# The order of a scan's loads in one DMA queue: the next pair's diagonals of B ahead of the present pair's C

## The reference

```python
x = x + 0.5 * ffn(layernorm(x))                 # y = xn @ int4(kernel) + bias + (xn @ a) @ b
x = x + mamba(layernorm(x))                     # below; it normalizes once more inside
x = x + 0.5 * ffn(layernorm(x))
# mamba, D_INNER = 512 channels d, D_STATE = 64 states s, 512 times t
x_ssm, z = split(h @ Win);  x_ssm = silu(conv4(x_ssm) + conv_b)
dt = softplus(x_ssm @ dt_w + dt_b);  A = -exp(A_log);  Bt = x_ssm @ Bp;  Ct = x_ssm @ Cp
state[d,s] = state[d,s] * exp(dt[t,d] * A[d,s]) + dt[t,d] * x_ssm[t,d] * Bt[t,s]
y[t,d] = sum_s state[d,s] * Ct[t,s]
out = x + ((y + x_ssm * D) * silu(z)) @ Wout
```

## Time and profile before

| | us |
|---|---|
| median of 3 runs | 5358.86 |
| the profiled execution | 5360.27 |
| its span, first to last instruction | 5358.5 |
| VectorE busy | 4882.4 (91%) |
| GpSimd busy | 5020.4 (94%) |
| TensorE busy, matmuls | 4832.5 (90%) |
| ACT busy | 3908.3 (73%) |
| 512 loads of C, median to landing | 5.3 |
| 512 loads of B, median to landing | 6.2 |

### The profile page before, as it was taken

One profiled execution on the slowest core, in us unless ns is written; L12 is line 12 of the kernel. 1 busy time (PEld: TensorE's weight loads), 2 busy tenths in 40 slices (PEclk: granted clock), 3 DMA queues, 4 the chain that ended last, 5 costly groups with the idle time before them and its releaser, 6 DMA issues.

```text
span 5358.5 us, 189344 instructions
## 1 busy us (share of the span) xinstructions
PE 4832.5 (90%) x85070; PEld 2903.5 (54%) x85070; DVE 4882.4 (91%) x4595; ACT 3908.3 (73%) x6661; POOL 5020.4 (94%) x2310
## 2 busy tenths in 40 slices
PE   4798989989999998989989999898999989899887
PEld 2455555555555555555555555555555555555554
DVE  1699999999999999999999999999999999999996
ACT  4767787777778677786777778777786777867564
POOL 0699999999999999999999999999999999999997
PEclk8899999999999999999999999999999999999999
DMA  6465665756556566665656556565665656557553
GB/s 174 161 170 192 180 185 190 177 199 180 188 185 182 192 171 202 179 184 189 180 197 181 189 179 181 197 172 194 183 176 192 173 198 171 190 183 180 187 188 115
DMA packets 578860, 976.04 MB, mean 182 GB/s; under 512 B 294881, under 2 KB 328450, under 8 KB 510466
## 3 DMA queue, kind: packets, MB, share of 16 engines
q1 hardware_dynamic: 313858, 961.82, 56.1%
q10 hardware_dynamic: 264192, 2.11, 3.4%
HBM read 875.74 MB, written 88.08 MB: 180 GB/s over the span
## 4 chain that ended last, share of the span: by engine, by line
PE 35%; POOL 26%; DVE 21%; issue 10%; ACT 4%; DMA 3%; SPq 0%; DVEq 0%; ACTq 0%; POOLq 0%
POOL H L618 23%; DVE H L528 18%; PE pUB L685 14%; PE Y L709 12%; PE pP L649 4%; PE pP L643 3%; DVE cv L479 2%; DMA Bd<-scratch_diag 2%; ACT dA L362 2%; PE pA L723 1%; POOL duo L605 1%; POOL dto L599 1%; POOL lnv L594 1%; ACT L362 1%; PE pA L729 1%
## 5 line engine op out<-in xcount | busy, mean ns | idle before, releaser
L618 POOL TENSOR_TENSOR H<-H,Cb 128x1024 f32<-128x1024 f32 x2048 | 4783.7, 2372 | 151.3 <-DVE H L528 141.9
L528 DVE TENSOR_TENSOR_SCAN H<-dA,pUB 128x512 f32<-128x512 f32 x4096 | 4640.1, 1199 | 244.1 <-PE pUB L685 219.8
L362 ACT ACTIVATE dA<-DT,w_negA 128x512 f32<-128x512 f32 x4096 | 2623.9, 713 | 1226.0 <-DVE H L528 1222.2
L685 PEld LDWEIGHTS pUB<-Bd,UT 64*64 64x64 f32 x65536 | 1867.5, 134 | 1439.1 <-DVE H L528 683.7
L685 PE MATMUL pUB<-Bd,UT 64*64 64x128 f32 x65536 | 2236.7, 275 | 413.3 <-DVE H L528 320.9
L709 PE MATMUL Y<-H,w_ident 64*64 64x512 f32 x16384 | 1971.2, 596 | 5.9 <-POOL H L618 4.9
L709 PEld LDWEIGHTS Y<-H,w_ident 64*64 64x64 f32 x16384 | 596.7, 135 | 611.1 <-issue 599.7
L643 PE MATMUL pP<-hT,w_Win 128*128 128x512 f32 x512 | 265.8, 643 | 19.8 <-DVE cv L479 12.6
L649 PE MATMUL pP<-U,w_dt_w 128*128 128x512 f32 x512 | 259.7, 631 | 5.1 <-DVE absv L542 3.7
L362 ACT ACT_TABLE_LOAD x178 | 228.4, 1283 | 6.5 <-DVE H L528 3.3
L479 DVE SCALAR_TENSOR_TENSOR cv<-pP,w_conv_w,cv 128x511 f32<-128x511 f32 (+2 forms) x192 | 139.2, 725 | 30.0 <-ACT cv L300 29.7
(11 more groups left out here) (80 smaller groups left out, 1745.1 us busy)
## 6 DMA issues: line engine op xcount, KB each, us to landing
Cb<-scratch_c SPq DMA_DIRECT2D x512, 1024.0 KB, 5.3
Bd<-scratch_diag SPq DMA_DIRECT2D x512, 512.0 KB, 6.2
scratch_diag<-H SPq DMA_DIRECT2D x16, 1024.0 KB, 15.2
scratch_z<-zo SPq DMA_DIRECT2D x64, 256.0 KB, 5.7
scratch_dt<-dto SPq DMA_DIRECT2D x64, 256.0 KB, 6.4
scratch_ut<-uto SPq DMA_DIRECT2D x64, 256.0 KB, 5.6
DT<-scratch_dt SPq DMA_DIRECT2D x64, 256.0 KB, 5.1
UT<-scratch_ut SPq DMA_DIRECT2D x64, 256.0 KB, 5.6
```

The costliest lines, as they stand in the source:

```text
L362: last = nc.scalar.activation(dA[:, n % DAR, j, :], DT[:, k, :], ACT.Exp, scale=c["negA"][:, k, GS * blk + j:GS * blk + j + 1])
L528: last = nc.vector.tensor_tensor_scan(H[:, u % HR, 2 * i + j, :], dA[:, n % DAR, 2 * i + j, :], pUB[:, i, :].rearrange("p (t s) -> p s t", ...
L618: nc.gpsimd.tensor_tensor(h[:, j:j + 2, :], h[:, j:j + 2, :], Cb[:, blk % 2, j:j + 2, :], ALU.mult).then_inc(times_c, 1)
L685: last = nc.tensor.matmul(out, UT[rows, k, j * P + h * HP:j * P + h * HP + HP], Bd[rows, blk % 2, i, j * P:(j + 1) * P].rearrange("p (t s) ...
```

## The change

load_block is split in two. load_b(b, seq + 1) stands where load_block stood, with the same wait, and asks for the next pair's diagonals. load_c(b, seq) stands behind it and asks for the C of the *present* pair; it waits until GpSimd has multiplied unit 2 * seq - 3, the last one that used that buffer, and that the batch's C has been stored (c_st). The C of the pass's last pair is asked for in step 62, and that of its first pair in step 0 rather than in step 62 of the pass before. The stores of dt move from steps 34, 40, 48, 56 to 35, 41, 49, 57, those of u from 42, 50, 58, 62 to 43, 51, 57, 63: odd steps, in which no B or C is loaded.

```diff
--- before.py
+++ after.py
@@ -29,7 +29,7 @@
 SPS = {"load x": (0,), "load 2": (10, 14), "load 0": (46, 54), "load r": (2,), "store z": (6, 12, 16, 22), "store C": (26,),
-       "store dt": (34, 40, 48, 56), "store u": (42, 50, 58, 62), "load z": (28, 29, 36, 37), "store out": (48,), "store r": (52,)}
+       "store dt": (35, 41, 49, 57), "store u": (43, 51, 57, 63), "load z": (28, 29, 36, 37), "store out": (48,), "store r": (52,)}
 ACTS = {"tap": (2, 7, 12, 17), "u": (5, 10, 15, 20), "z": (5, 10, 15, 20), "BC": (24,), "B": (26,),
         "store B": (27, 28, 29, 32, 33, 34, 35, 38), "dt": (30, 36, 44, 52), "log": (31, 37, 45, 53), "turn u": (40, 48, 56, 61),
         "keep u": (57, 59), "norm 1": (3, 4, 6, 11), "norm c": (22, 23, 26, 29), "norm 2": (39, 42, 43, 47, 49),
@@ -207,13 +207,18 @@
                                      w["Win"][:, DI + ch:DI + ch + HP].rearrange("(k p) m -> p k m", p=P)).then_inc(k_big, 16)
                         sp.dma_start(c["Wout"][side:side + HP, tile, :], w["Wout"][ch:ch + HP, :]).then_inc(k_big, 16)
-            def load_block(b, seq, units):
+            def load_b(b, seq, units):
                 blk = seq % NBLK
                 sp.wait_ge(forced, at(2 * units))
                 diag = dram["diag"][bass.ds(b % 2, 1), (2 * blk + 1) * EL:(2 * blk + 3) * EL].rearrange("o (i p f) -> p (o i) f", p=P, f=T)
                 sp.dma_start(Bd[:, seq % 2], diag).then_inc(d_in[seq % 2], 16)
-                sp.wait_ge(times_c, at(2 * units))
+
+            def load_c(b, seq):
+
+                blk = seq % NBLK
+                sp.wait_ge(c_st, at(16 * b + 16))
+                sp.wait_ge(times_c, at(2 * (GN * b + 2 * seq - 2)))
                 rows = dram["c"][bass.ds(b, 1), GS * blk + 1:GS * (blk + 1) + 1, :].rearrange("o s t -> o (s t)")
                 sp.dma_start(Cb[:, seq % 2].rearrange("p s t -> p (s t)"), rows.to_broadcast([P, GS * T])).then_inc(c_in[seq % 2], 16)
@@ -252,7 +257,9 @@
                         sp.wait_ge(x1_done, at(2 * a))
                         sp.dma_start(X[:, :, :], tokens_of("x", a)).then_inc(x_in, 16)
                     if scan and n % 2 == 0 and seq < 2 * NBLK - 1:
-                        load_block(b, seq + 1, GN * b + n)
+                        load_b(b, seq + 1, GN * b + n)
+                    if scan and n % 2 == 0:
+                        load_c(b, seq)
                     if scan and n in when["load 2"]:
                         load_du(b, 2 + when["load 2"].index(n))
                     if close and n in when["load r"]:
@@ -283,8 +290,7 @@
                         load_du(q, when["load 0"].index(n))
                     if proj and n == GN - 2:
                         sp.wait_ge(d_st, at(16 * 2 * NJ * (q + 1)))
-                        sp.wait_ge(c_st, at(16 * q + 16))
-                        load_block(q, 0, GN * q - 2)
+                        load_b(q, 0, GN * q - 2)
             sp.dma_start(X[:, :, :], tokens_of("x", 0)).then_inc(x_in, 16)
             constants()
```

## The result

The changed kernel is slower. Its runs take 5403.65 to 5438.38 us, median 5431.77, against 5359.90 for four runs before; the ratio is 1.0132, 95% interval 1.0097 to 1.0168. The forecast was 5367, "no change that can be told", in a range that ended at 5412. The profiled execution of the changed kernel (5403.65 us) is the quickest of its runs, with a granted clock of 0.977; the others have 0.970 to 0.972.

A forecast was written before the change was run, and what follows sets the result against it. GpSimd's work and the scan were taken to bound the kernel by turns. Per pass, -1.9 us (B(0) sooner) and +2.4 (GpSimd late at unit 38) gave +0.5, over 15 joints +7.5: 5367 us, range 5322 to 5412.

The forecast's parts named there:

- no change that can be told: Whole kernel: the forecast outcome, 5367 us, own range 5340 to 5390, chance 0.50.
- Item 1: Late units: B leaves before C's wait, closing VectorE holes such as 1.58 us at unit 60; worth nothing by itself.
- the sign in the prediction, under 30: Profile after the change: TensorE's waits for B were to fall from 119 us to under 30.
- Item 2: Start of the next pass: B(0) asked for and landing sooner, 1.9 us a pass gained, bounds 0.5 and 3.7.
- Item 3: Units 8 to 38: C behind B is 1.5 us late, free there; C(19) costs 0.8 us at unit 38.
- Item 4: Units 27 to 35, among diagonals' stores: C late 4.5 us, 2.1 worked off, 2.4 left at unit 38.
- They don't add, the greater holds: At unit 38: of the 2.4 us lag and C(19)'s 0.8 us only the larger counts.
- Item 5: Stores of dt and u at their new steps: 0 us, bounds -0.3 and +0.5 us a pass.
- Late C wins: Slower rival: C(14) to C(17) late in units 28 to 34, 3.3 us a pass, 5409 us; chance 0.29 with its kin.
- its own sign: Sign of the slower rival: GpSimd begins unit 38 over 4 us after that unit's first two scan rows.
- The new wait of VectorE behind TensorE's sums: Sign at L709 that the forecast's ground is wrong: GpSimd's lag would have reached VectorE; no size given.

The follow-up runs named there:

- e8: e7 with the next pass's B(0) (first diagonals) asked for ahead of C(31), the pass's last C; 5319.03 us, ratio 0.9895 to the kernel before.
- e7: Changed kernel with C behind the next B only for pairs 0 to 2 and 24 to 31, other C a pair ahead; 5354.60 us, ratio 0.9965.
- e3: Changed kernel with the eighth store of B's diagonals moved from step 38 to step 42; 5435.96 us, ratio 1.0113.
- r1: The changed kernel run and profiled again, unaltered, on another chip; 5459.44 us, ratio 1.0153.
- e2: Kernel before with only the new steps of the dt and u stores, old order of the loads; 5382.77 us, ratio 1.0014.
- e9: Changed kernel with the next pass's B(0) asked for ahead of C(31); 5399.58 us, ratio 1.0053.
- e10: Kernel before with one difference, the next pass's B(0) asked for ahead of C(31); 5376.45 us, ratio 1.0000.
- e5: Changed kernel with all eight stores of B's diagonals moved to steps 39 to 46; 5474.06 us, ratio 1.0181.

## Why the prediction was wrong, point by point

- *Item 1, B no longer behind C's wait, worth nothing by itself: right as far as it goes.* The 119 us of the earlier trace rows are waits of TensorE's weight loads; its matmuls waited 65.7 us for B, some 8 of them in front of unit 64. (In the pass that the prediction read, it took TensorE to be held by its own work, since the row says "issue"; B(0) landed 0.1 us before TensorE's start there, too.) After, the waits in front of the other units are gone and those in front of unit 64 are 50 us: the sign in the prediction, under 30, failed. The lead brings VectorE to unit 63 4.3 us sooner. Its main use comes with e8's swap, where it is worth 3.4 us a pass (joint 1 of e7 against e8).
- *Item 2, B(0) sooner, 1.9 us a pass: the size right, the parts not.* Joint 1 gained 1.6 to 1.7 us (8.8 to 7.15, 7.1). The request is 0.5 us sooner, as computed, but the landing only 0.8 us and not 1.5; the rest is VectorE's lead, which the item had named for some of the passes.
- *Item 3, C late in the quiet part: its size right there, wrong at unit 38.* From B's request 6.8 us, as computed. But "There the room is from 2943.70 to 2949.70, 6.0 us, and C(19) lands after 6.8: 0.8 us" took the quiet price in a place where the eighth store of diagonals goes out 1.05 us ahead of B(20). The prediction's own text spoke of "seven of eight from unit 27 to 35" and gave the eighth, at step 38, no price. Measured: lands at 11.1 to 11.6, not 6.8 (e3, without the store: 7.4). This is the step that failed.
- *Item 4, lag from the stores' part: 2.4 us at unit 38 predicted, 3.5 and 3.3 measured* (after, r1) as GpSimd's end of unit 37 (9.2 and 9.0 against 5.7). The start was mis-sized by little: GpSimd is 5.9 us behind the scan at unit 28 (before 0.6, medians), so 5.3 against 4.5. What was wrong is the working off: I counted 2.1 us of before's idle time as free for it, but new waits for C fill part of it (0.54 and 0.80 us above, at units 30 and 32). At unit 36 it is still 5.3 us behind (before 0.4).
- *"They don't add, the greater holds":* so far right; joint 2 is the later of the two. But the greater was C(19), and joint 2 4.8 to 5.5 us later than before, not 2.4.
- *Item 5, the stores' steps, 0: right* (e2, at the edge of its interval).
- *A term that was missing: TensorE's clock.* Nothing in the sum stood for what its idle time in front of unit 64 brings. Nine of the 14 passes of after have the stretch, at 2.3 us each: 1.5 us a pass. In the profiled execution this took back a gain rather than adding a loss: up to unit 28 after takes 145.4 us, the kernel before 145.7. In r1 it is 146.3.
- *The rivals.* "Late C wins", 5409, was the nearest, and its own sign came: GpSimd begins unit 38 5.1 us after its first two scan rows, over the 4 us that it named (0.2 before). Its lag at unit 28, 5.8 us, was met too. By e3 that lag makes some 3.3 us of joint 2; the rest is C(19), which it did not have. Its net 3.3 us a pass agrees with the 3.2 of the profiled execution, with other parts; that is in part luck.

The sum as measured in the profiled execution: -1.6 + 4.8 = +3.2 us a pass, where -1.9 + 2.4 = +0.5 was forecast. That is the 43 us. The other 28 us between it and the median come with a lower clock (0.971 against 0.977) and have no trace of their own. r1, at the same clock, has a scan 3 us longer than after's; 0.9 of that fits the stretches behind TensorE's idle time, and the 2.1 in units 28 to 37 stay open.

The new wait of VectorE behind TensorE's sums appeared too, at unit 59, VectorE and TensorE of after:

```profile
3073.12 5.67 DVE L534 TENSOR_TENSOR_SCAN H<-dA,pUB 128x512 f32<-128x512 f32 x5 [4.65 <-PE pUB L691]
```

```profile
3067.56 3.69 PE L715 MATMUL Y<-H,w_ident 64*64 64x512 f32 x16 [2.38 <-POOL H L624]
3071.03 3.20 PE L691 MATMUL pUB<-Bd,UT 64*64 64x128 f32 x64
```

It lies where GpSimd, not the scan, sets the time, so it costs nothing by itself; the matmuls behind it ran slow as well (3.69 us for 16 that take 1.90, at a granted clock of 0.50 from 3067.4 to 3071.3).

What stays open: why e8's and e9's scans are some 2 us longer than that of the kernel before (194.0 to formed 37) with 5.9 and 4.6 us of slow time against 4.6 (1.9 and 1.3 us of it lie in units 28 to 37); why r1's is longer there than after's, with the same program; and why VectorE is later at unit 63 in e2.

## What to carry to other kernels

When two loads share a queue and change places, price the one that is now second at every handover between limits, with everything that starts on any queue within some microseconds of it: the same 1 MB took 4.8 us alone, 6.3 behind 0.5 MB, and 10.8 to 12 among stores of 8-byte pieces. A load that comes sooner pays only up to the next thing that is late: B(0) alone sooner (e10) met VectorE, the other B alone sooner (e7) met B(0), and both together (e8) took 4.9 us off joint 1. The reordering lost 1.3 to 1.5%, one more swap took two thirds of that back, and the early C kept in the pairs where GpSimd has no backlog made 1.05% of gain out of it. And an idle moment of TensorE costs more than itself if its clock falls after it, here some 2 us each time.

## What the runs showed of the hardware

- After 2.4 to 5.0 us without work TensorE's granted clock fell to 1.2 GHz for a stretch of 3.4 us (0.52 in the one shown) in 10 of 15 passes of after and in all 15 of r1 (twice for 6.8 us); after 2.1 to 3.8 us in the other five of after it did not. In e8 and e9, with no idle time in front of unit 64, there was no such stretch. 64 matmuls took 3.50 us instead of 2.12, and such a pass was 2.3 us longer at unit 28 (after).
- Eight stores a pass of 16 KB each, in 8-byte pieces, are 3.1% of the DMA engines' time in after, but lengthen a 1 MB load near them by 3 us (9.3 in that part against 6.3) to 5.7 us (12.0 in e5).
- The same kernel took 5432 us on one chip and 5459 on another, the kernel before 5360 and 5376. The ratios, 1.0132 and 1.0153, agree within their intervals.
